# Cross-attention on one core: the softmax maximum taken in two parts

## The reference

```python
C_q = Q @ Wq_d
C_kv = K @ Wkv_d
CqWqk = (C_q @ W_qk).reshape(b, n, H, LKV)
scores = jnp.einsum('bnhl,bkl->bhnk', CqWqk, C_kv) / jnp.sqrt(LKV)
attn = jax.nn.softmax(scores, axis=-1)
V_up = (C_kv @ Wv_u).reshape(b, nkv, H, HD)
out = jnp.einsum('bhnk,bkhd->bnhd', attn, V_up)
```

## Time and profile before

| What | Value |
|---|---|
| three runs | 2830.6 us median (2820.8 to 2831.57) |
| profiled execution, first to last instruction | 2825.3 us |
| attention's first maximum starts, last one ends | 368.0 us, 1494.3 us |
| 430 to 1500 us: PE, DVE, ACT, POOL busy of 1070 us | 1008.49, 880.21, 809.13, 780.57 us |
| same stretch: granted TensorE clock, DMA share | 0.99, 0.72 |

### The profile page before, as it was taken

How to read it: one execution, slowest core, us unless ns; L and a number is a source line. 1 busy time by engine, 2 the same in 40 slices (tenths; PEclk the granted TensorE clock), 3 DMA queues, 4 the chain that set the end, 5 groups by cost and what they waited for, 6 DMA issues and landing times. The chain is left out here.

```text
span 2825.3 us, 41267 instructions
## 1 busy us (share of the span) xinstructions
PE 2646.3 (94%) x14360; PEld 1994.5 (71%) x14360; DVE 2262.4 (80%) x2150; ACT 1680.2 (59%) x2635; POOL 1940.3 (69%) x1423
## 2 busy tenths in 40 slices
PE   6988989999999999999997999999999999999997
PEld 3655656666666666666665788888888888788885
DVE  1644668888887788778875899999999899899988
ACT  2343567777777777777775554445445555555553
POOL 1000457767777777767774888888887788888883
PEclk9888989999999999999998999999999999999999
DMA  7224766766677677677764222221222222232221
GB/s 257 94 91 154 229 221 204 231 193 203 205 230 219 210 213 219 209 234 232 227 203 141 105 90 93 86 75 68 69 78 96 95 88 84 67 120 75 75 97 75
DMA packets 166768, 420.60 MB, mean 149 GB/s; under 512 B 30113, under 2 KB 57634, under 8 KB 166050
## 3 DMA queue, kind: packets, MB, share of 16 engines
q1 hardware_dynamic: 164258, 409.57, 46.4%
q10 hardware_dynamic: 2304, 8.39, 0.7%
HBM read 248.43 MB, written 75.04 MB: 114 GB/s over the span
## 5 line engine op out<-in xcount | busy, mean ns | idle before, releaser
L1656 DVE SCALAR_TENSOR_TENSOR c_acc<-c_ps,c_sd,c_acc 128x1024 f32<-128x1024 f32 x448 | 573.1, 1282 | 95.2 <-PE c_ps L1503 95.1
L1233 POOL COPY b_pt<-b_tn 32x640 f32<-32x640 f32 x640 | 457.0, 714 | 268.6 <-DVE b_tn L1135 236.9
L1561 ACT ACTIVATE c_scaled<-c_ps,c_sgu 128x1024 f32<-128x1024 f32 x336 | 375.3, 1117 | 420.8 <-PE c_ps L1503 418.8
L1129 DVE TENSOR_REDUCE b_nm<-b_sc 128x1 f32<-128x1604 f32 x256 | 468.1, 1828 | 190.5 <-PE b_sc L964 189.3
L1046 ACT ACTIVATE b_pr<-b_sc,b_nm 128x799 f32<-128x799 f32 (+1 forms) x512 | 476.5, 933 | 240.3 <-DVE b_nm L1129 215.8
L1743 POOL TENSOR_TENSOR c_sum_u<-c_sum_u,c_scaled 128x1024 f32<-128x1024 f32 x168 | 404.7, 2409 | 107.9 <-ACT c_scaled L1561 107.5
L1743 POOL TENSOR_TENSOR c_sum_g<-c_sum_g,c_scaled 128x1024 f32<-128x1024 f32 x168 | 405.1, 2411 | 81.9 <-ACT c_scaled L1561 81.7
L964 PE MATMUL b_sc<-b_kh,b_qs 128*128 128x402 f32 (+1 forms) x1024 | 404.4, 395 | 41.1 <-ACT b_pr L1046 37.4
L983 PE MATMUL b_po<-b_pt,shared 128*64 128x256 f32 x2560 | 392.3, 395 | 32.5 <-DMA b_pt<-b_tn 32.4
L1135 DVE STREAM_TRANSPOSE b_tn<-b_pr 128x1280 f32<-128x1280 f32 x256 | 384.8, 1503 | 6.8 <-DMA b_pt<-b_tn 2.9
L964 PE MATMUL b_sc<-b_kl,b_qs 128*128 128x402 f32 (+1 forms) x1024 | 358.6, 350 | 0.0
(11 more groups left out here) (194 smaller groups left out, 4387.3 us busy)
## 6 DMA issues: line engine op xcount, KB each, us to landing
b_pt<-b_tn SPq DMA_DIRECT2D x1152, 80.0 KB, 2.6
c_uw_int<-wint_u SPq DMA_DIRECT2D x56, 512.0 KB, 3.5
c_gw_int<-wint_g SPq DMA_DIRECT2D x56, 512.0 KB, 3.4
c_dw_int<-wint_d SPq DMA_DIRECT2D x56, 512.0 KB, 3.4
a_cx<-in_b_ctxT SPq DMA_DIRECT2D x16, 1608.0 KB, 10.1
b_rw<-in_c_gw SPq DMA_DIRECT2D x28, 512.0 KB, 4.2
b_rz<-in_c_gz SPq DMA_DIRECT2D x28, 512.0 KB, 5.5
b_rw<-in_c_uw SPq DMA_DIRECT2D x28, 512.0 KB, 4.0
```

Of the source, the lines that this page charges most:

```text
L1129: V.tensor_reduce(nm[:, u % 2:u % 2 + 1], both, AXY, ALU.max, negate=True).then_inc(s_nm, 1)
L1233: G.tensor_copy(pt[s][32 * c:32 * c + 32, a, :, :], tn[s][32 * a:32 * a + 32, c, :, :]).then_inc(s_block, 1)
L1561: S.activation(dst[:, :], pair[SLOT[x, t] % 4][:, :], ACT.Identity, scale=scale(x, t)).then_inc(s_e, 1)
L1656: V.scalar_tensor_tensor(out=total, in0=pair[SLOT[x, t] % 4][:, :], scalar=scale(x, t), in1=total, op0=ALU.mult, op1=ALU.add).then_inc(s_a ...
```

## The change

The maximum over half 0 of a unit is taken in an instruction of its own (`first_maximum`), which is issued one step ahead: that of unit k+1 stands behind `turn(k-1)` in step k. `maximum(k)` now reads half 1 alone, 799 scores, with a tensor-scalar instruction: it multiplies by -1, takes the minimum with the first part's result (a per-partition scalar), and its accumulator gives the minimum over the row, the negated maximum of the whole unit. Its elementwise result is not used; it goes to the probability tile of the unit, where the exponential of half 1 later writes. For that, `maximum` also waits for the semaphores of the block transpose and of TensorE's transposes of unit k-2, which read this tile; and for the first part's own semaphore. Two semaphores of the mixer become one, counted to 2.

```diff
@@ attention
+        s_part = sem("nm_part")
+        nm0 = sb("b_nm_first", [P, 2])
@@ vector
+            def first_maximum(u):
+                at = half_at(u, 0)
+                V.wait_ge(s_sc, 2 * u + 1)
+                V.tensor_reduce(nm0[:, u % 2:u % 2 + 1], sc[:, at + SIDE[0][0]:at + SIDE[0][1]], AX, ALU.max,
+                                negate=True).then_inc(s_part, 1)
             def maximum(u):
-                first, second = half_at(u, 0) + SIDE[0][0], half_at(u, 1) + SIDE[1][0] - 3
+                at, j = half_at(u, 1), slice(u % 2, u % 2 + 1)
                 V.wait_ge(s_sc, 2 * u + 2)
+                V.wait_ge(s_part, u + 1)
                 if u >= 2:
                     V.wait_ge(s_ex, 2 * u - 2)
-                both = bass.AP(sc, min(first, second), [[3 * 1024, P], [abs(second - first), 2], [1, 802]])
-                V.tensor_reduce(nm[:, u % 2:u % 2 + 1], both, AXY, ALU.max, negate=True).then_inc(s_nm, 1)
+                    V.wait_ge(s_tr, u - 1)
+                    V.wait_ge(s_tt, u - 1)
+                V.tensor_scalar(pr[u % 2][:, SIDE[1][2]:SIDE[1][3]], sc[:, at + SIDE[1][0]:at + SIDE[1][1]], -1.0, nm0[:, j],
+                                ALU.mult, ALU.min, accum_out=nm[:, j]).then_inc(s_nm, 1)
...
+            first_maximum(0)
             for k in range(NU + OUT_AT):
                 if k < NU:
                     maximum(k)
...
                 if 1 <= k <= NU:
                     turn(k - 1)
+                if k + 1 < NU:
+                    first_maximum(k + 1)
                 if k < NU:
                     norm_piece(k)
```

More of the change, by code:

```diff
@@ L80, in mixer @@
         s_down, s_gelu, s_xmid = sem("down"), sem("gelu"), sem("xmid")
-        s_clamp, s_aexp, s_gexp, s_ones, s_half, s_prep = (sem(n) for n in ("clamp", "aexp", "gexp", "ones", "half", "prep"))
+        s_clamp, s_gates, s_ones, s_half, s_prep = (sem(n) for n in ("clamp", "gates", "ones", "half", "prep"))
         s_z, s_sz, s_dt = sem("z"), sem("sz"), sem("dt")
@@ L388, in scalar @@
             S.wait_ge(s_clamp, 1)
-            S.activation(alog[:, :], alog[:, :], ACT.Exp).then_inc(s_aexp, 1)
-            S.activation(g1[:, :], g1[:, :], ACT.Sigmoid).then_inc(s_gexp, 1)
+            S.activation(alog[:, :], alog[:, :], ACT.Exp).then_inc(s_gates, 1)
+            S.activation(g1[:, :], g1[:, :], ACT.Sigmoid).then_inc(s_gates, 1)
             S.wait_ge(s_xmid, L)
@@ L553, in vector @@
             V.tensor_single_scalar(alog[:, :], alog[:, :], 85.0, ALU.min).then_inc(s_clamp, 1)
-            V.wait_ge(s_aexp, 1)
+            V.wait_ge(s_gates, 1)
             V.tensor_scalar(alog[:, :], alog[:, :], -1.0, None, ALU.mult)
-            V.wait_ge(s_gexp, 1)
+            V.wait_ge(s_gates, 2)
             V.tensor_scalar(gates[:, 0:1], g1[:, :], 1.0, 1.0, ALU.mult, ALU.add)
```

## The result

The kernel with the change takes 2807.2 us (median of 4 runs, 2804.6 to 2807.9) beside 2827.2 us for the kernel before (4 runs, 2820.8 to 2831.6): a ratio of 0.9921, 95% interval 0.9905 to 0.9937. The forecast was 2816, with a range of 2790 to 2840. The profiled spans, 2825.3 before and 2805.7 after, differ by 19.6 us. Nearly all of it (19.4) lies in the attention stage: from the first scores of half 1 to the last it takes 1125.0 us before and 1105.6 after.

What follows compares the result with a forecast made beforehand. A ring of PE, DVE and ACT bounded five of eight attention steps, PE's own work the other three. Span 2825.3 - 40 (ring) + 5 (statistics) + 21 (exchange) = 2811; the runs' median is 5.3 above, so 2816 us, range 2790 to 2840.

Steps and rivals of the forecast that it cites:

- The ring: Attention's loop of PE's scores, DVE's maximum and ACT's exponential, 4.06 us a step; shortening it was to gain 40 us.
- W7: Attention step kind, three of five ring-bound steps in eight; to fall from 4.06 to PE's own 3.94 us, gaining 0.12.
- W6: Attention step kind, two of five ring-bound steps in eight; to gain 0.45 of a possible 0.68 us, ending at 3.5 to 3.7.
- the long steps: Three of eight attention steps, with the projection or an output, set by PE's own work: 4.84, 4.44 and 4.28 us.
- The group of eight: Eight consecutive attention steps, 33.85 us before; forecast 32.6 where no block is late, 1.26 less, over 32 groups.
- the read: DVE's reading out of the tensor-scalar's accumulator, taken as 0.1 us added on the ring.
- the walk: Step-by-step timing of a W7 step and the W6 step behind it, giving gains of 0.12 and 0.45 us.
- the statistics: Layer-norm work on DVE behind the first part, delaying the tensor-scalar some 0.4 us in 12 W6 steps: 5 us lost.
- The exchange: SP's queue of DMAs exchanging the pairs' blocks; making PE wait more, it was to take back 21 us, from nothing to 40.
- the exchange takes all, or nothing: Rivals: first, SP's queue and DMA landings take the whole gain, 2825 to 2832 (0.27); second, whole gain stays, 2796 (0.20).
- VectorE as the bound: Rival, chance 0.13: DVE limits attention steps; slower above a tensor-scalar of about 1.45 us, 2869 us at 1.6.
- The rule against the change: Skill's rule that DVE's next operation waits for an empty pipe: W6 steps end 0.1 to 0.16 us later, time 2826.

Runs made afterwards that it cites:

- e9: The changed kernel with only 4 of the 84 feed-forward weight blocks loaded, prepared and stored during attention; 2758.7 us, ratio 0.9740 to the kernel before.
- e10: The kernel before the change with the same cut to 4 of 84 weight blocks in the attention; 2801.7 us, ratio 0.9888 to the kernel before.
- e1: The changed kernel with one of each pair's nine exchange DMAs copied by GpSimd instead; 2792.7 us, ratio 0.9861 to the kernel before.
- e4: The changed kernel with the layer norm's statistics ahead of the first part in VectorE's list; 2808.6 us, ratio 0.9918 to the kernel before.
- e5: The changed kernel with eight exchange DMAs, a sixth block on GpSimd and the weight-block store after the fourth DMA; 2801.5 us, ratio 0.9878.
- e8: The changed kernel with seven exchange DMAs, seven blocks on GpSimd and the weight-block store after the fourth DMA; 2799.6 us, ratio 0.9880.

## Why the prediction was right

**The ring.** Mechanism and pieces as predicted: tensor-scalar 1.05, W7 3.91 to 3.94 for 3.94, W6 3.54 and 3.63 for 3.6, and the long steps stayed (4.88 and 4.44). The group of eight is 32.46 for 32.6: a gain of 1.39 instead of 1.26, since the third long step (4.21 for 4.28) and the second W6 step gave a little more. One term was too large: the read was priced at 0.1 on the ring, but it overlaps the tensor-scalar and ends 0.01 after it, so the exponential starts 1.18 us after the tensor-scalar's start (848.94 to 850.12) where the walk has 1.27. The shorter group gives 0.13 x 32 = 4 us, most of the distance between the span predicted (2811) and found (2805.7). Net of the statistics 35 us were forecast, and e9 with e10 measured 43 (40.3 in their profiles).

**The statistics.** In the traces of e1 and e9 each of the twelve W6 steps that hold statistics is 0.15 to 0.39 us longer than the median step at its place in the eight, 3.7 us in all, for 0.4 each and 5 in all predicted. e4 shows that their order costs nothing more.

**The exchange.** Predicted 21 us taken back, found 23 (43 less 20) by experiment and 25 by the steps (29 less some 4 of the statistics); PE's wait for blocks at 65 or more, found 69.1; SP's wait for the transposes to fall, 65.6 to 51.5. That stretches of stores stay at SP's pace is seen (10.5 and 10.7 us). The experiments show that the weight stream is what makes the blocks late. They do not part SP's queue from the landing of the DMAs and from GpSimd: e9 relieves them all, and e5 to e8, meant to free SP alone, made other transfers late. The traces of after and e9 do part them, in the mean. From the end of a pair's second transpose to the landing of its last exchange DMA are 8.93 us in after and 7.45 in e9 (means over the pairs 8 to 119). Of the 1.48 us SP's later start is 0.49 (0.53 and 0.04), its slower issuing of the nine 0.55 (6.44 and 5.89), and the later landing behind the last issue 0.44 (1.96 and 1.52): about a third each. GpSimd's copies end before the last DMA lands in every one of these pairs, ScalarE's in all but six. That the forecast's sum came so near is partly luck: it let each of 43 waits grow by 0.31 us and some 30 new ones come, and found are 56 waits, 13 more, with a mean of 1.23 us beside 1.09.

**The miss.** ACT's wait for the maximum was to shrink by more than half and went from 196.8 to 143.0. The step that failed is the reading of the earlier trace rows: I took that wait for the ring's slack. But where PE is the bound, ACT must be idle, and the profile puts that idle to the last thing that came: 1.57 us at 858.28, in a W7 step that is PE's own 3.91. PE's wait for ACT, 69.8 to 33.2, was the measure of the ring.

**The rivals.** That the exchange takes all, or nothing, is refuted by the 20 of 43 us left. The first was the nearer to the truth in its mechanism, and a choice of half was right for a stage where SP was waiting in half of the exchanges. VectorE as the bound needed a tensor-scalar of 1.45; it is 1.05. The rule against the change (2826) had no overlap behind the extra instruction, and the trace has 0.07 us.

## What to carry to other kernels

When a reduction stands in a ring, ask which of its inputs come early: taking that part ahead can gain although it adds instructions (20 us), and the same split without being ahead loses (63 us). Work out the next bound step by step before counting the gain, here PE's own work, ACT's copies and the queue of the exchange; and measure what a change is worth with the suspected taker removed from both kernels (43 beside 20 us). Judge a ring by the waits of the engine that sets the end, not by those of the engines that serve it.

## What was not expected of the hardware

The tensor-scalar with an accumulator takes 1050 ns for 799 columns of PSUM, only 0.07 us more than the 0.98 to which the plain copies extrapolate, and reading out its accumulator takes 83 ns on DVE where ACT's takes 199. The nine DMA issues of one exchange held SP for 7.6 us twice in the earlier trace rows; in after the same nine took 5.57 to 8.54 us in neighbouring pairs, so their price is not fixed: in e9, with hardly any weight blocks beside them, the median is 5.58 us, in after 6.38.
